# An attention layer with its heads padded on the key side: GpSimd pads K, Q is one dense add, the causal mask joins the maximum on VectorE

## The chip, the cores and the metric

The kernel runs on one core of one Trainium2 chip. The metric is the time of one execution on the device, in microseconds (us); lower is better. Five engines run their own queues of instructions in order: TensorE (PE, with its weight loads shown as PEld), VectorE (DVE), ScalarE (ACT), GpSimd (POOL) and SyncE (SP), which issues most DMAs. They meet at semaphores.

## What is computed

A residual stream `x` of 4 batches of 1024 tokens of 128 features goes through six layers: mixture of experts, a two-way state-space layer, mixture of experts, a ternary gated network, causal attention, the ternary network again. The change is inside the attention layer alone. Cut to what matters, that layer is

```python
# x: 4 batches, 1024 tokens, 128 features; 16 heads of 8 features
q, k, v = split(layernorm(x) @ w_in.T + b_in)      # each to heads: (batch, 16, 1024, 8)
scores = einsum('bhqd,bhkd->bhqk', q / sqrt(8), k) + causal_bias   # 0 or -inf
out = einsum('bhqk,bhkd->bhqd', softmax(scores), v)
x = x + out.reshape(batch, 1024, 128) @ w_out.T + b_out
```

All of it is in float32; the projections are taken in three matmul passes with the operands split into a rounded high part and a low rest.

## The kernel before, in words

The attention layer is the function `attention` (L1781). It handles the 16 heads in 4 groups of 4 heads, batch after batch: 16 group turns in all, and a turn is called a slot here. A head has 8 features, and its row block on the 128 partitions is 32 rows: 8 rows of the rounded part, 8 twice for the rest, and rows that carry the row maximum. Four heads together fill 128 rows, so a matmul over 128 rows would mix the four heads. To keep them apart one of the two operands holds zeros in the rows of the other three heads. In the kernel before that operand is Q: `Q` has one 1024-column block per head (16 of them), `K` has one dense block per group.

A slot is 12 steps (`STEPS`), v = 0 to 11. Each step has four units, one a head:

- PE's `exp_unit` (L2008, matmul L2018) makes the transposed scores of group g into one of three PSUM buffers, ACT's `exp_unit` (L2109, L2116) takes the exponential, POOL's `mask_step` (L2354, L2357 and L2360) zeroes the triangle in the eight steps on the diagonal (v = 0 to 3 and 8 to 11), and PE's `value_step` (L2022, L2034) of the step before multiplies by V, between the second and third unit.
- The pass for the row maximum of the next group runs beside it: PE's `max_unit` (L1994, matmul L2002) makes scores into one of three other buffers, DVE's `max_unit` (L2207, L2216) reduces them. On the diagonal chunks, 32 of the 48 units of a slot, a second matmul (L2005) adds -1e30 above the diagonal: identity times mask, 128 columns. A PE unit waits until the third unit before it has been read by ACT or DVE.
- After its four units a step may have one further use of the single PSUM bank `M` (`slot_uses` L1812, `m_use` L2037): at v = 0 and 2 the projection of Q of the group after next, at 4 and 5 that of K, at 6 that of V, at 1 and 7 the transposed row maxima ("max"), at 3 and 9 the normalisation of the output. A use waits until the one before has been read out of `M`.

Q and K come out of `M` as two ACT instructions (`qf` L2135, `qh` L2138) and one on DVE (`stack`, L2283). K lands dense in `K`. Q lands in the scratch `stk`, and ACT's `queries` (L2147, L2155) copies it to the padded `Q`: four instructions of 32 partitions for each half of 512 columns, placed in the steps v = 9 and 10, one after each exponential. The zeros of `Q` are written once ahead of the layer: by one POOL memset (L2332) and three DMAs (L2330). "max" adds the row maxima to `Q`, in the DVE function `m_read` (L2225): four instructions of 32 partitions x 512 (L2238), two between each pair of units of steps 2 and 8.

The order on each engine is written out by `all_slots` (L1897): a stage "pre" that has the maximum pass of group 0 only, a stage "first" for batch 0, a loop `Fori` for batches 1 and 2, "last" for batch 3, and "tail". Before the slots POOL fills constants and computes two reciprocal roots (`rstd_of`, L2322).

## Time and profile before

| | us |
|---|---|
| time, median of 3 runs | 2952.7 (2952.65 to 2961.28) |
| span of the profiled execution | 3037.0 |
| attention layer in it, without its tail | 1973.0 to 2757.5 |
| of that, the pass for the first maximum | 2002.4 to 2034.0 |
| the 16 slots | 2034.0 to 2757.5 |
| PE, DVE, ACT, POOL busy over the whole span | 2549.4, 2285.1, 1790.3, 1373.7 |

The profile gives no time of that execution beyond its span, so what lies around the span is in no row; the comparison goes span against span and median against median. Times in the trace are counted from the start of the span. A duration that a row shows is that of an instruction from its start to its end; instructions of one engine overlap a little, so that the distance from start to start is shorter. A busy PE is a modelled time. "Idle before, releaser" tells how long an engine stood still before an instruction and what it was that ended the wait.

### The profile page before, as it was taken

To read this page: it belongs to the slowest core of one execution; us is meant where nothing else is said; L and a number is where in the kernel's file an instruction comes from. 1 tells how busy PE (TensorE), PEld (TensorE's weight loads), DVE (VectorE), ACT (ScalarE), POOL (GpSimd) and SP (SyncE) were. 2 spreads that over 40 slices of the span, in tenths; PEclk is the share of its full clock that TensorE was granted. 3 is DMA by queue.
4 is the path that set the end of the run, shared out by engine and by line. 5 is a ranking of instruction groups with operands and counts; after the bars stand their busy time and mean duration, and the time that the engine had idled before them with its cause. 6 is when DMAs were issued, how large, how long until landed. Compare 5 with 4: busy or idle time off the path is not lost. (4 is left out here: it accounts for less than half of the span.)

```text
span 3037.0 us, 38397 instructions
## 1 busy us (share of the span) xinstructions
PE 2549.4 (84%) x11128; PEld 1669.2 (55%) x11128; DVE 2285.1 (75%) x3877; ACT 1790.3 (59%) x3099; POOL 1373.7 (45%) x1486
## 2 busy tenths in 40 slices
PE   6888477888888888868887689969988889887999
PEld 5766233343344344227676568746555556554887
DVE  6887478989999999998786544478777777774444
ACT  3566465657556656524666445547777667665555
POOL 2365488888988988961563630021121121111000
PEclk9999688999999999998998789979999999998999
DMA  2246222222222222221345200020000000001000
GB/s 69 55 130 123 79 68 67 75 69 72 70 74 74 77 73 74 77 71 39 75 130 96 73 21 1 0 95 1 1 1 1 2 1 1 1 1 39 7 8 14
DMA packets 99804, 152.38 MB, mean 50 GB/s; under 512 B 12940, under 2 KB 50572, under 8 KB 99028
## 3 DMA queue, kind: packets, MB, share of 16 engines
q1 hardware_dynamic: 82052, 98.41, 10.6%
q0 software_dynamic: 17040, 51.07, 6.8%
q8 instruction: 91, 1.49, 0.2%
q14 instruction: 109, 0.89, 0.1%
q10 hardware_dynamic: 512, 0.53, 0.1%
HBM read 131.08 MB, written 18.87 MB: 49 GB/s over the span
## 5 line engine op out<-in xcount | busy, mean ns | idle before, releaser
L1750 POOL TENSOR_TENSOR a_hc<-a_H,a_cb 128x512 f32<-128x512 f32 x512 | 620.0, 1233 | 134.3 <-DVE a_H L1614 127.3
L1406 PE MATMUL a_Y<-a_hc,ident 128*128 128x512 f32 x1024 | 535.3, 633 | 57.0 <-POOL a_hc L1750 48.6
L2216 DVE TENSOR_REDUCE a_mx<-a_W 128x1 f32<-128x512 f32 (+3 forms) x768 | 397.2, 550 | 153.3 <-PE a_W L2005 99.6
L2116 ACT ACTIVATE a_pt<-a_W 128x512 f32<-128x512 f32 (+3 forms) x768 | 353.5, 493 | 224.1 <-PE a_W L2018 220.7
L1532 ACT ACTIVATE a_dA<-a_dt,a_aneg 128x512 f32<-128x512 f32 x512 | 342.6, 714 | 193.8 <-POOL a_dt L1769 103.2
L1406 PEld LDWEIGHTS a_Y<-a_hc,ident 128*128 128x128 f32 x1024 | 183.0, 196 | 307.6 <-POOL a_hc L1750 212.7
L1638 DVE TENSOR_TENSOR a_BX<-a_u,a_BX 128x1024 f32<-128x1024 f32 x256 | 308.6, 1211 | 44.0 <-PE a_BX L1340 22.3
L1614 DVE TENSOR_TENSOR_SCAN a_H<-a_dA,a_H,a_BX 128x512 f32<-128x512 f32 x256 | 312.5, 1264 | 2.5 <-ACT a_dA L1532 2.5
L2018 PE MATMUL a_W<-a_Q,a_K 128*128 128x512 f32 (+3 forms) x768 | 302.3, 399 | 4.1 <-ACT a_pt L2116 2.0
L1614 DVE TENSOR_TENSOR_SCAN a_H<-a_dA,a_BX 128x512 f32<-128x512 f32 x256 | 296.7, 1202 | 1.1 <-POOL a_hc L1750 1.0
L2002 PE MATMUL a_W<-a_K,a_Q 128*128 128x512 f32 (+3 forms) x768 | 273.9, 363 | 20.4 <-DVE a_K L2283 9.9
L2357 POOL TENSOR_TENSOR a_spare<-a_zero 128x1 f32<-128x1 f32 x128 | 27.8, 217 | 578.9 <-ACT a_pt L2116 578.9
L1340 PE MATMUL a_BX<-a_bcs,a_sel 128*128 128x512 f32 x256 | 173.9, 680 | 96.4 <-DVE a_H L1614 82.6
L715 POOL DMA_INDIRECT m_xg<-m_xrows,m_gidx x184 | 190.1, 1033 | 120.9 <-DVE m_didx L599 65.4
L1046 DVE TENSOR_TENSOR t_hl<-t_raw,t_hh 128x512 fp32r<-128x512 f32 x128 | 87.5, 691 | 203.1 <-ACT t_hh L947 184.2
L2018 PEld LDWEIGHTS a_W<-a_Q,a_K 128*128 128x128 f32 x768 | 145.8, 192 | 142.0 <-issue 68.8
L441 ACT ACTIVATE m_raw<-m_U,m_wg 128x512 f32<-128x512 f32 x248 | 172.6, 697 | 82.6 <-PE m_U L335 48.0
L609 DVE TENSOR_TENSOR m_hl<-m_raw,m_hh 128x512 fp32r<-128x512 f32 x248 | 171.1, 692 | 56.4 <-ACT m_hh L445 30.7
L2034 PE MATMUL a_PV<-a_pt,a_V 128*32 128x512 f32 (+3 forms) x1536 | 167.0, 507 | 42.4 <-POOL a_pt L2360 41.3
L842 PE MATMUL t_U<-t_hh,t_wh 128*128 128x512 f32 x512 | 201.4, 393 | 0.0
L844 PE MATMUL t_U<-t_hl,t_wh 128*128 128x512 f32 x512 | 199.5, 390 | 0.0
L843 PE MATMUL t_U<-t_hh,t_wl 128*128 128x512 f32 x512 | 199.3, 389 | 0.0
(327 smaller groups left out, 5628.4 us busy)
## 6 DMA issues: line engine op xcount, KB each, us to landing
a_cb<-a_crow SPq DMA_DIRECT2D x256, 256.0 KB, 3.1
m_orows<-m_yt SPq DMA_DIRECT2D x46, 256.0 KB
a_Q<-attention_zeros POOLq DMA_DIRECT2D x3, 2048.0 KB, 13.3
t_wst<-ternary_w SPq DMA_DIRECT2D x22, 256.0 KB, 2.7
m_xrows<-m_pool SPq DMA_DIRECT2D x16, 256.0 KB, 2.3
m_xg<-m_xrows,m_gidx POOLq DMA_INDIRECT x184
out<-x SPq DMA_DIRECT2D x8, 256.0 KB, 2.3
m_wg<-moe_ws SPq DMA_DIRECT2D x2, 516.0 KB, 4.5
```

The source lines that it names most:

```text
L842: pe.matmul(out, wh[:, piece, c], rhs_h, start=start, stop=False)
L843: pe.matmul(out, wl[:, piece, c], rhs_h, start=False, stop=False)
L844: return pe.matmul(out, wh[:, piece, c], rhs_l, start=False, stop=stop)
L1406: pe.matmul(Y[:, h, :], ident[:], hc[:, g % HCRING, :], start=False, stop=v == NS - 1).then_inc(s_y, 1)
L1532: act.activation(dA[:, G % ARING, :], dt[:, b % 2, h, :], ACT.Exp, scale=aneg[:, d, h, v:v + 1]).then_inc(s_dA, 1)
L1614: dve.tensor_tensor_scan(out, a, bb, init, ALU.mult, ALU.add).then_inc(s_scan, 1)
L1638: dve.tensor_tensor(both_banks(Q), u[:, b % 2, :, :], BX[:, row_bank(Q), :].unsqueeze(1).broadcast_to([P, HALF, BLK]), ALU.mult).then_inc( ...
L1750: pool.tensor_tensor(hc[:, G % HCRING, :], H[:, s, span], cb[:, v % RING, :], ALU.mult).then_inc(s_hc, 1)
L2002: mm = pe.matmul(out, Q[:, g * GH + j, tile(t)], K[:, g, c * BLK:c * BLK + cols], start=True, stop=not diag)
L2018: pe.matmul(W[:, 3 + u % 3, 0:BLK - r * P], K[:, g, tile(kt)], Q[:, g * GH + j, c * BLK + r * P:(c + 1) * BLK], start=True, stop=True).the ...
L2116: act.activation(pt[:, u % PR, 0:BLK - r * P], W[:, 3 + u % 3, 0:BLK - r * P], ACT.Exp).then_inc(s_exp, 1)
L2216: dve.tensor_reduce(dst, W[:, s % 3, 0:min(BLK, (t + 1) * P - c * BLK)], AX, ALU.max)\
```

## The change

The two operands swap roles. `K` becomes the padded one (16 blocks) and `Q` the dense one (4 blocks).

- The projection order swaps: K at v = 0 and 2, Q at v = 4 and 5. K now goes through `stk`, Q lands in `Q`.
- POOL pads K: for each half of 512 columns four `tensor_scalar` of 128 x 512, each multiplying `stk` by a column that is 1 in the rows of one head and 0 elsewhere, and by 1.0. They stand after the masks of steps 2 and 3 (two each, the first half) and after the split of the next group's maxima (four, the second half). Eight of them stand in POOL's queue before it splits the first maxima, and eight more for group 1.
- ACT's copies L2155 go. The memset L2332 and the DMAs L2330 go.
- "max" is one DVE add of 128 x 512 to `Q` instead of four of 32 x 512.
- On the diagonal the second matmul L2005 goes. DVE adds the mask and takes the maximum in one `tensor_tensor_reduce`, which also writes the masked scores to a scratch `masked`. The mask is loaded 512 columns wide (384 of zeros before the triangle) instead of 128. Off the diagonal DVE's `tensor_reduce` stays.
- The `Fori` loop becomes a Python loop: batches 1 and 2 are written out.

The diff, cut to its core:

```diff
-            uses.update({-7: ("xT", 0, 0, 0), -6: ("xT", 0, 0, 1), -5: ("Q", 0, 0, 0), -4: ("Q", 0, 0, 1),
-                         -3: ("K", 0, 0, 0), -2: ("K", 0, 0, 1), -1: ("V", 0, 0, 0)})
+            uses.update({-7: ("xT", 0, 0, 0), -6: ("xT", 0, 0, 1), -5: ("K", 0, 0, 0), -4: ("K", 0, 0, 1),
+                         -3: ("Q", 0, 0, 0), -2: ("Q", 0, 0, 1), -1: ("V", 0, 0, 0)})
...
-            uses.update({0: ("Q", rel, n, 0), 2: ("Q", rel, n, 1), 4: ("K", rel, n, 0), 5: ("K", rel, n, 1),
+            uses.update({0: ("K", rel, n, 0), 2: ("K", rel, n, 1), 4: ("Q", rel, n, 0), 5: ("Q", rel, n, 1),
...
-        with eng.Fori(1, NBATCH - 1) as i:
+        for i in range(1, NBATCH - 1):
...
-                    out = W[:, s % 3, 0:cols]
-                    mm = pe.matmul(out, Q[:, g * GH + j, tile(t)], K[:, g, c * BLK:c * BLK + cols],
-                                   start=True, stop=not diag)
-                    if diag:
-                        mm = pe.matmul(W[:, s % 3, cols - P:cols], idr[:], mneg[:], start=False, stop=True)
-                    mm.then_inc(s_S, 1)
+                    pe.matmul(W[:, s % 3, 0:cols], Q[:, g, tile(t)], K[:, g * GH + j, c * BLK:c * BLK + cols],
+                              start=True, stop=True).then_inc(s_S, 1)
...
-                    pe.matmul(W[:, 3 + u % 3, 0:BLK - r * P], K[:, g, tile(kt)],
-                              Q[:, g * GH + j, c * BLK + r * P:(c + 1) * BLK],
+                    pe.matmul(W[:, 3 + u % 3, 0:BLK - r * P], K[:, g * GH + j, tile(kt)],
+                              Q[:, g, c * BLK + r * P:(c + 1) * BLK],
...
-                                    pe.wait_ge(s_q, 2 * G + 4)
+                                    pe.wait_ge(s_k, 2 * G + 4)
...
-                            copied = copies(stage, g, v)
-                            if copied:
-                                queries(i, copied, j)
...
+                    if last:
+                        dve.tensor_tensor_reduce(masked[:, s % 3, 0:cols], W[:, s % 3, 0:cols], mask[:, BLK - cols:],
+                                                 1.0, LEAST, ALU.add, ALU.max, dst).then_inc(s_max, 1)
+                    else:
+                        dve.tensor_reduce(dst, W[:, s % 3, 0:cols], AX, ALU.max).then_inc(s_max, 1)
...
-                    if kind == "max" and j < 2:
-                        for jj in (2 * j, 2 * j + 1):
-                            q = Q[head(jj), n * GH + jj, chunk(c)]
-                            ins = dve.tensor_tensor(q, q.bitcast(F32), M[head(jj), :], ALU.add)
-                        if j == 1:
-                            last = ins
+                    if kind == "max" and j == 0:
+                        q = Q[:, n, chunk(c)]
+                        last = dve.tensor_tensor(q, q.bitcast(F32), M[:], ALU.add)
...
-                for dst, src in ZEROS:
-                    pool.dma_start(dst, src).then_inc(s_zero, 16)
                 pool.wait_ge(s_xn, 1)
-                pool.memset(Q[:, 0:GH, :].bitcast(F32), 0.0).then_inc(s_cst, 1)
...
+                def keys(G, n, c, js):
+
+                    if js[0] == 0:
+                        pool.wait_ge(s_ld, 16 * len(LOADS))
+                        pool.wait_ge(s_st, 4 * G + c + 1)
+                    for j in js:
+                        last = pool.tensor_scalar(K[:, n * GH + j, chunk(c)], stk[:, c, :].bitcast(F32),
+                                                  heads[:, j:j + 1], 1.0, ALU.mult, ALU.mult)
+                    if js[-1] == GH - 1:
+                        last.then_inc(s_k, 1)
+
                 def slot(stage, i, g):
                     G = i * GROUPS + g
+                    n = (g + 2) % GROUPS
+                    ahead = stage not in ("last", "tail") or (stage == "last" and g + 2 < GROUPS)
+                    if stage == "pre":
+                        keys(0, 0, 0, range(GH))
+                        keys(0, 0, 1, range(GH))
+                        keys(1, 1, 0, range(GH))
+                        keys(1, 1, 1, range(GH))
                     if has_exp(stage):
                         split_max(stage, i, g, G, g, 1)
                         for v in DIAG[:TPB]:
                             mask_step(i, g, v)
+                            if ahead and v >= 2:
+                                keys(G + 2, n, 0, range(2 * (v - 2), 2 * (v - 1)))
                     if has_max(stage, g):
                         split_max(stage, i, g, G + 1, (g + 1) % GROUPS, 0)
                     if has_exp(stage):
+                        if ahead:
+                            keys(G + 2, n, 1, range(GH))
                         for v in DIAG[TPB:]:
                             mask_step(i, g, v)
```

## Rows read from the trace of the kernel before

**Rows 1.** First maximum pass: stretch, us, busy PE, PEld, DVE, ACT, POOL, clock, DMA.
```profile
2002.40:2034.00 31.60, 27.58 (x109) 20.68 (x109) 28.38 (x59) 11.98 (x17) 0.99 (x3) 0.75 0.00 1
```

**Rows 2.** The same view of two single slots, the seventh and the eighth.
```profile
2306.20:2350.30 44.10, 39.69 (x267) 26.30 (x265) 34.89 (x71) 32.66 (x67) 8.28 (x22) 1.00 0.01 2
2350.30:2397.00 46.70, 40.39 (x266) 26.60 (x264) 35.52 (x72) 32.45 (x67) 9.85 (x27) 0.96 0.01 2
```

**Rows 3.** Waits in the 16 slots: waiter, releaser: us in total, times, longest.
```profile
PEld a_W L2018 <- ACT a_pt L2116: 62.8, 92, 1.2
PEld a_PV L2034 <- POOL a_pt L2360: 58.6, 70, 1.5
PEld a_M L1990 <- DVE a_Q L2238: 17.1, 14, 2.2
```

**Rows 4.** Groups of DVE by shape: busy us, mean ns, idle before.
```profile
L2216 DVE TENSOR_REDUCE a_mx<-a_W 128x1 f32<-128x512 f32 x384 | 247.4, 680 | 74.6 <-PE a_W L2002 50.5 <-PE a_W L2005 23.6
L2238 DVE TENSOR_TENSOR a_Q<-a_Q,a_M 32x512 fp32r<-32x512 f32 x128 | 87.2, 681 | 8.2 <-PE a_M L2063 6.3
L1614 DVE TENSOR_TENSOR_SCAN a_H<-a_dA,a_BX 128x512 f32<-128x512 f32 x256 | 296.7, 1202 | 1.1 <-POOL a_hc L1750 1.0
L2283 DVE SCALAR_TENSOR_TENSOR a_stk<-a_qh,a_low,a_qf 128x512 f32<-128x512 f32 x32 | 28.4, 887 | 1.8 <-ACT a_qh L2138 1.4
L2222 DVE TENSOR_TENSOR a_mx<-a_mx 128x4 f32<-128x4 f32 x64 | 12.0, 187 | 1.0
```

**Rows 5.** Groups by shape on ACT, PE and POOL.
```profile
L2155 ACT ACTIVATE a_Q<-a_stk 32x512 fp32r<-32x512 f32 x128 | 80.1, 626 | 5.7 <-DVE a_stk L2283 3.1
L2005 PE MATMUL a_W<-a_mneg,a_idr 128*128 128x128 f32 x512 | 123.3, 241 | 0.0
L2360 POOL TENSOR_SCALAR_AFFINE_SELECT a_pt<-a_pt 128x512 f32<-128x512 f32 x128 | 87.2, 681 | 0.0
L1750 POOL TENSOR_TENSOR a_hc<-a_H,a_cb 128x512 f32<-128x512 f32 x512 | 620.0, 1233 | 134.3 <-DVE a_H L1614 127.3 <-PE a_Y L1406 6.0
```

**Rows 6.** Timeline of DVE: start, us (all of the row's instructions), what.
```profile
2314.22 1.36 DVE L2238 TENSOR_TENSOR a_Q<-a_Q,a_M 32x512 fp32r<-32x512 f32 x2
2315.91 1.39 DVE L2238 TENSOR_TENSOR a_Q<-a_Q,a_M 32x512 fp32r<-32x512 f32 x2
...
2390.14 2.48 DVE L2216 TENSOR_REDUCE a_mx<-a_W 128x1 f32<-128x512 f32 x4 [0.57 <-PE a_W L2002]
```

**Rows 7.** Timeline of PE, pieces of the seventh slot; the last row opens the ninth.
```profile
2316.14 0.22 PE L2002 MATMUL a_W<-a_K,a_Q 128*128 128x128 f32 x1
2316.20 0.27 PE L2005 MATMUL a_W<-a_mneg,a_idr 128*128 128x128 f32 x1
2317.36 0.50 PE L1990 MATMUL a_M<-a_xh,a_wh 128*128 128x512 f32 x1 [0.89 <-DVE a_Q L2238]
...
2340.62 1.06 PE L2034 MATMUL a_PV<-a_pt,a_V 128*32 128x512 f32 x8
...
2344.65 0.85 PE L2034 MATMUL a_PV<-a_pt,a_V 128*32 128x384 f32 x8 [0.76 <-POOL a_pt L2360]
...
2345.89 0.28 PE L2018 MATMUL a_W<-a_Q,a_K 128*128 128x256 f32 x1
...
2348.73 0.64 PE L2034 MATMUL a_PV<-a_pt,a_V 128*32 128x256 f32 x8 [1.24 <-POOL a_pt L2360]
...
2397.04 0.79 PE L2018 MATMUL a_W<-a_Q,a_K 128*128 128x512 f32 x1 [1.94 <-issue]
```

**Rows 8.** Timeline of ACT in steps 9 and 10 of the seventh slot.
```profile
2342.09 0.49 ACT L2116 ACTIVATE a_pt<-a_W 128x384 f32<-128x384 f32 x1 [0.73 <-PE a_W L2018]
...
2343.25 0.49 ACT L2116 ACTIVATE a_pt<-a_W 128x384 f32<-128x384 f32 x1
...
2347.43 0.39 ACT L2116 ACTIVATE a_pt<-a_W 128x256 f32<-128x256 f32 x1
```

**Rows 9.** Timeline of POOL ahead of the slots.
```profile
1992.98 4.20 POOL L2326 TENSOR_TENSOR a_rstd<-a_veps,a_mhalf 128x24 f32<-128x24 f32 x1
```

More of the change, by code:

```diff
@@ L1795, in attention @@
     ROWS = P // GH
+    LEAST = -3.0e38
     NCH, TPS = SEQ // BLK, SEQ // P
@@ L1846, in attention @@
             for st, gs in SLOTS.items()}
-    def copies(stage, g, v):
-        uses = slot_uses(stage, g)
-        use = uses.get(v - 2) if v < 0 else uses.get({9: 0, 10: 2}.get(v))
-        return use if use and use[0] == "Q" else None
     WEIGHT = {"M": lambda k: 1, "D": lambda k: k not in ("Q", "K", "oT"), "A": lambda k: k in ("Q", "K", "oT"),
@@ L1920, in attention @@
         wo, bo = sb("wo", [P, P]), sb("bo", [P, P])
-        mask = sb("mask", [P, P])
-        idr, mneg = sb("idr", [P, P], F32R), sb("mneg", [P, P], F32R)
-        stk = sb("stk", [P, 2, BLK])
+        mask, heads = sb("mask", [P, BLK]), sb("heads", [P, GH])
+        masked = sb("masked", [P, 3, BLK])
+        stk = sb("stk", [P, 2, BLK], F32R)
         mhalf, zero = sb("mhalf", [P, TILES]), sb("zero", [P, TPB, GH])
@@ L1961, in attention @@
                  (scale[:], w["scale"]), (low[:], w["low"]), (wo[:], w["w_out"]), (bo[:], w["b_out"]),
-                 (mask[:], w["mask"]))
-        ZEROS = tuple((Q[:, n:n + GH, :].rearrange("p h c -> p (h c)"), w["zeros"].bitcast(F32R))
-                      for n in range(GH, GROUPS * GH, GH))
+                 (mask[:], w["mask"]), (heads[:], w["heads"]))
         def early(v):
@@ L2097, in slot @@
                             m_use(stage, i, g, v, uses[v])
-                all_slots(slot, pe)
+                all_slots(slot)
             @block.scalar
@@ L2105, in _ @@
                 act.activation(wvh[:], wvs[:], ACT.Copy).then_inc(s_wh, 1)
-                act.activation(idr[:], ident[:], ACT.Copy)
-                act.activation(mneg[:], mask[:], ACT.Copy).then_inc(s_pre, 1)
                 def exp_unit(i, g, v, j):
@@ L2145, in m_read @@
                             act.activation(oT[:, c, :], M[:], ACT.Copy).then_inc(s_Ma, 1)
-                def queries(i, use, j):
-                    if isinstance(i, int) and i == 0 and use[2] == 1 and j == 0:
-                        act.wait_ge(s_zero, 16 * len(ZEROS))
-                    kind, rel, n, c = use
-                    G = (i + rel) * GROUPS + n
-                    if j == 0:
-                        act.wait_ge(s_st, 4 * G + c + 1)
-                    last = act.activation(Q[head(j), n * GH + j, chunk(c)], stk[head(j), c, :], ACT.Copy)
-                    if j == GH - 1:
-                        last.then_inc(s_q, 1)
                 def slot(stage, i, g):
@@ L2275, in stack @@
                     G = (i + rel) * GROUPS + n
-                    m, k = (c, n) if kind == "Q" else (2 + c, GROUPS + n)
+                    m, k = (c, GROUPS + n) if kind == "K" else (2 + c, n)
                     dve.wait_ge(s_Ma, through("A", stage, i, g, v))
-                    if kind == "Q":
-                        wait(dve, s_q, 2 * (G - 1) + c + 1)
+                    if kind == "K":
+                        wait(dve, s_k, 2 * (G - 1) + c + 1)
                         out = stk[:, c, :]
                     else:
-                        out = K[:, n, chunk(c)]
+                        out = Q[:, n, chunk(c)]
                     dve.scalar_tensor_tensor(out, qh[:, m % 2, :].bitcast(F32), low[:, k:k + 1],
@@ L2313, in _ @@
                 chain = [None]
-                all_slots(slot, dve)
+                all_slots(slot)
             @block.gpsimd
@@ L2525, in attention_layout @@
         "w_out": g("w_out").T, "b_out": np.broadcast_to(g("b_out"), (P, P)),
-        "mask": np.triu(np.full((P, P), -1e30, np.float32), 1), "zeros": np.zeros((P, 4096), np.float32),
+        "mask": np.pad(np.triu(np.full((P, P), -1e30, np.float32), 1), ((0, 0), (3 * P, 0))), "heads": np.repeat(np.eye(GH, dtype=np.float32), ROWS, 0),
     }
```

27 lines of the change are left out of this document (12 added, 15 removed).

## The prediction

> **What bounds the kernel now.** Nothing outside the attention layer changes, so only its 784 us count, and of these the 16 slots are 723.5 us. I read busy time by stretch first. In a slot of 44.1 us PE is busy 39.7, DVE 34.9, ACT 32.7 and POOL 8.3 [rows 2]. No engine is full, PE is nearest, and its clock is at the upper of its levels, 2.4 GHz, for the whole slot. So the slot is a chain that runs through the engines in turn, and the waits tell where PE stands still. Over the 16 slots it waits 62.8 us for ACT's exponentials, 58.6 for POOL's triangle mask, which follows them, and 17.1 for DVE's adds to Q, in 14 places [rows 3]. The timeline shows the two places:
>
> - In step 2 the last mask matmul starts at 2316.20 and the next projection at 2317.36, because DVE needs until 2317.3 for four adds with reductions between them [rows 6, 7].
> - In steps 9 and 10 the value matmuls wait for POOL's mask; POOL waits for the step's fourth exponential, and that one stands on ACT behind copies of Q, one after each exponential [rows 5, 7, 8].
>
> **The change part by part.** All prices are per slot and from start to start where the rows allow it.
>
> *Mask matmuls.* 32 go. The next matmul starts 0.06 us after a 128-column one [rows 7], so they cost PE 32 x 0.057 = 1.8 us; the 0.241 us of the group is length, not cost [rows 5]. Half of them (steps 0, 1, 3, 6) stand where PE never waits: 0.9 us kept. The others lie in the waits counted next.
>
> *The adds to Q.* Four instructions of 0.68 us become one of 128 x 512; its DVE time goes by the columns, not by the partitions, so it is priced like one of the four [rows 4, 6]. DVE gets back 2 x 3 x 0.69 = 4.1 us. On the path: bank M is read at 2314.22 + 0.68 = 2314.90 instead of 2317.30. The projection of step 2 then follows its last score matmul at about 2316.26: 1.1 us kept. In step 8 the same adds hold a score matmul, but the value matmul behind it waits for POOL's mask anyway, which comes from exponentials that are not touched: 0.3 us kept.
>
> *ACT's copies.* Eight of 0.626 us go [rows 5], 5.0 us of ACT. On the path: in step 9 the fourth exponential starts 2343.25 and the third 2342.09. Without the copy between them it starts 0.5 later than the third, at 2342.6: 0.65 us earlier, and with it mask and value matmul (2344.65). In step 10 the fourth exponential starts at 2347.43, though its scores were started at 2345.89. The lag from score matmul to exponential without a queue is about 0.47 (2341.62 is the score matmul's start after the value matmul of 2340.62 and its 1.0 us; the exponential follows at 2342.09 [rows 7, 8]), so it could start at 2346.36. That is 1.07 earlier, and the value matmul of 2348.73 moves with it. What comes late next there is DVE: four reductions take 2.48 us [rows 6], and between two value matmuls there are four of them and the small operations of the normalisation, 2.9 us, against the 3.0 that the chain then takes. So these are kept, but no more. Sum 1.7 us.
>
> *The fused instruction.* 32 reductions become `tensor_tensor_reduce`, and the trace has no such instruction. From below: nothing extra, since a two-operand DVE instruction of 512 columns takes 681 ns and a reduction 680 [rows 4]. From above: the scan, also a two-operand instruction with a running result, takes 1202 ns at the same width. I take 0.10 us extra for each, near the lower end, because a running maximum is what the reduction does already, four of 512 columns in 2.48 us [rows 6]. That is 3.2 us of DVE, less than the 4.1 that the adds give back. It hides in DVE's idle time (9 us a slot), except in steps 9 to 11 and at chain ends: 0.5 us lost.
>
> *POOL's padding.* Eight instructions of 128 x 512 with one tensor input. Bounds: the triangle mask, one input, 0.68 us, and a product of two tensors, 1.23 us [rows 5]. I take 0.75, near the one-input row: 6 us, on an engine busy 8.3 of 44.1 us. Queued behind the first two, and behind their wait for `stk`, is the mask of step 3, on which PE's value matmul waits. `stk` is written by the end of step 1 and padded after the mask of step 2, so that wait is over before it starts. The masks of steps 2 and 3 are ready some 3.5 us apart; two paddings take 1.5, so nothing. The other six fall between steps 3 and 8, when POOL has nothing else but the split of the maxima, used at step 7 at the earliest: nothing. If a padding took 1.23, the mask of step 3 would be up to 0.7 us late.
>
> Sum for a slot: 0.9 + 1.1 + 0.3 + 1.7 - 0.5 = 3.5 us. It holds for the 14 slots that have projections and copies: 49.0 us. The fifteenth has neither and keeps 1.0, the last has no maximum pass and keeps about 1.1 through the adds.
>
> *The loop.* The eighth slot ends with the loop's back edge. It takes 46.7 us instead of 44.1, and PE stands 1.94 us at the start of the ninth for nothing that the profile shows [rows 2, 7]. The clock is 0.96 there, so part is the clock's. Bounds 1.9 and 4.2 (the slow first step after it included); I take 3.0. Entering the loop costs nothing visible, and batches 0 and 3 are straight code already with slots of the same length, so fetching more code is put at nothing.
>
> *Ahead of the slots.* The memset, the zero DMAs and ACT's eight copies go, but POOL's queue now holds the first keys: its reciprocal roots end at 1997.2 [rows 9], and eight paddings of 0.75 put the first score matmul at 2003.2, against 2002.4 now: 1.0 lost (range 0 to 4.7). The first maximum pass is DVE's own, 28.4 of 31.6 us [rows 1]: 32 x 0.10 added, three adds of 0.69 and the lag of the mask matmuls taken away, 0.5 lost. The larger mask to load may delay the first projections by under 1 us; they wait later for the statistics anyway.
>
> Total: 49.0 + 1.0 + 1.1 + 3.0 - 1.0 - 0.5 = 52.6 us. Against the profiled execution that is 3037.0 - 52.6 = 2984 us of span. That execution is 2.8% longer than the median; the difference is taken over unscaled, as scaling it would change it by 1.5 us: 2952.7 - 52.6 = 2900 us.
>
> **Rivals.**
>
> *The fused instruction costs like two.* The nearest row for a second small instruction is the 4-column maximum, 187 ns [rows 4]. Then DVE gets 6.0 us more in a slot against 4.1 less, and 1.5 instead of 0.5 us come to lie on the path; the first pass loses 2.9 more. 2900 + 14 + 3 = 2917. For it: the instruction has two results. The Trainium skill says just this, in "VectorE: DVE Perf Modes", section "Two Vector instructions with no wait between them": an operation that also writes out its accumulator is two instructions, the main one and the read of the accumulator. No row here shows such a pair.
>
> *GpSimd is slow.* 1.23 us a padding: 14 x 0.7 + 8 x 0.48 = 14 us, 2914. Against it: the mask, also one input, takes 0.68.
>
> *The fused instruction runs at half rate (slower than before).* Priced like the scan it costs 0.58 us more at 512 columns, and by the 10240 diagonal columns of a slot 11.6 us: DVE has 34.9 - 4.1 + 11.6 = 42.4 us of work, bunched where the diagonal units are wide. Steps 11, 0 and 1 have 4 x 1.2 + 4 x 1.2 + 4 x 0.9 = 13.2 us of it against 10.9 that these steps last, and what the other steps gain is eaten by DVE's starts behind the value matmuls. I put the slot at 45.6, 1.5 more than now, which is 22 us; the first pass 6.5 more; the loop 3.0 less: 2978. It decides from about 1.1 us for 512 columns. For it: the scan's row [rows 4]. Against it: the reduction runs at full rate. The Trainium skill stands against it too, in "DVE: opcode table, instruction layouts, handler registers and perf-mode slots", section 6: a stage that reads its own last result has no bubble, and only a result carried back to an earlier stage, as in the scan, halves the rate; the 1202 and 680 ns of the two rows agree.
>
> *The freed time is idle time.* PE is 90% busy, and what DVE and ACT no longer do may only lengthen their waits; then the kernel keeps the loop and some mask matmuls, 8 us in all: 2945. Against it: the two chains above are seen, wait by wait.
>
> **How the numbers follow.** Forecast 0.58; a gain beyond it (nothing for the fused instruction, all mask matmuls kept, the loop at 4.2: 4.9 us a slot, 2870) 0.04; two instructions 0.13; GpSimd slow 0.12; half rate 0.08, of which 0.01 ends near no change; idle time 0.05. A measurement of this kernel tells 0.3%, 8.9 us, from no change. Faster 0.87, same 0.06, slower 0.07. Range: low 2868, the case beyond; high 2930, two instructions and slow padding together. Outside it are the half rate and the idle case.
>
> **What would show it.** In the profile after: the step-2 projection directly behind the last score matmul; `exp` back to back in steps 9 and 10 and PE's waits for POOL down from 58.6 to some 30 us; the fused instruction within 0.7 to 0.8 us at 512 columns; a padding at 0.65 to 0.85; first score matmul near 2003; slots of 40 to 41 us. Wrong if the fused instruction takes over 0.9 us, if PE's waits for POOL grow, or if slots stay at 44.

## The result and the profile after

The changed kernel takes 2872.9 us (median of 4 runs, 2870.1 to 2875.5), the kernel before 2955.3 beside it: ratio 0.972, 95% interval 0.971 to 0.974. That is 82.4 us less, where 52.6 were forecast. The time lies inside the range (2868 to 2930), at its low end.

The profiled execution of before was longer than its median, and the excess lies in the stages ahead of attention, which take about 84 us more in it and in every run of two of the three sets of experiments below, whatever the kernel; so only stretches within attention are compared here, and experiments are set against a kernel that ran beside them.

Within attention the stages read as follows. The start, from GpSimd's first memset to the first score matmul, went from 28.7 to 30.3 us (1.7 lost, 1.0 forecast). The first maximum pass went from 31.6 to 29.5 (2.1 gained, 0.5 lost was forecast). The 16 slots went from 723.5 to 641.3: 82.2 gained. In this view the rows are the first maximum pass, the seventh slot, the eighth, and all sixteen; the first three answer to [rows 1, 2].

```profile
1916.06:1945.60 29.54, 25.75 (x77) 16.48 (x77) 26.40 (x87) 7.07 (x9) 5.98 (x11) 0.73 0.00 0
2191.30:2230.90 39.60, 36.87 (x235) 22.21 (x234) 30.26 (x97) 27.30 (x59) 13.61 (x30) 1.00 0.01 1
2230.90:2270.20 39.30, 36.55 (x234) 22.14 (x233) 29.57 (x96) 26.96 (x59) 13.83 (x30) 1.00 0.00 1
1945.60:2586.90 641.30, 583.86 (x3697) 352.22 (x3695) 466.31 (x1476) 426.43 (x923) 206.88 (x460) 0.99 0.00 1
```

The seventh slot lost 4.5 us of its 44.1. PE is now busy 36.9 of 39.6, DVE 30.3 (34.9 before), ACT 27.3 (32.7), and POOL 13.6 (8.3), which has taken the padding. The eighth is shorter by 7.4, since the loop's back edge has gone with it.

The groups of DVE and POOL that answer to [rows 4, 5]:

```profile
L2186 DVE CUSTOM_DVE_ANT_0 a_masked<-a_W,a_mask 128x512 f32<-128x512 f32 x128 | 82.8, 686 | 9.5 <-PE a_W L1991 8.0
L2186 DVE DVE_READ_ACCUMULATOR2_ANT a_mx<- 128x1 f32 x512 | 42.2, 82 | 0.0
L2189 DVE TENSOR_REDUCE a_mx<-a_W 128x1 f32<-128x512 f32 x256 | 166.7, 680 | 50.4 <-PE a_W L1991 48.0
...
L2335 POOL TENSOR_SCALAR a_K<-a_stk,a_heads 128x512 fp32r<-128x512 f32 x128 | 86.5, 691 | 7.9 <-DVE a_stk L2252 7.8
L2326 POOL TENSOR_SCALAR_AFFINE_SELECT a_pt<-a_pt 128x512 f32<-128x512 f32 x128 | 95.3, 744 | 0.0
```

The fused instruction has a second record, the read of its accumulator. Whether that costs anything is read from starts, not from durations. DVE's timeline, around the seam of the seventh and the eighth slot (start, us):

```profile
2229.22 0.68 DVE L2186 CUSTOM_DVE_ANT_0 a_masked<-a_W,a_mask 128x512 f32<-128x512 f32 x1
2229.83 0.08 DVE L2186 DVE_READ_ACCUMULATOR2_ANT a_mx<- 128x1 f32 x1
2229.83 0.69 DVE L2186 CUSTOM_DVE_ANT_0 a_masked<-a_W,a_mask 128x512 f32<-128x512 f32 x1
2230.44 0.08 DVE L2186 DVE_READ_ACCUMULATOR2_ANT a_mx<- 128x1 f32 x1
```

The next fused instruction starts in the same hundredth as the read, 0.61 us after the one before it. Plain reductions of this width follow each other at 0.60 to 0.62 (four in 2.48 in [rows 6]). So the mask is free on DVE, to 0.01 us. The same holds at 128, 256 and 384 columns, where the shortest distances from start to start are 0.21, 0.34 and 0.47 us here and 0.20, 0.33 and 0.46 for the reduction before.

PE's and ACT's timelines in the seventh slot, and POOL's ahead of the slots, which answer to [rows 7 to 9]:

```profile
2200.70 0.22 PE L1991 MATMUL a_W<-a_K,a_Q 128*128 128x128 f32 x1
2200.75 0.45 PE L1981 MATMUL a_M<-a_xh,a_wh 128*128 128x512 f32 x1
...
2223.32 1.06 PE L2020 MATMUL a_PV<-a_pt,a_V 128*32 128x512 f32 x8 [0.74 <-POOL a_pt L2326]
...
2229.43 0.64 PE L2020 MATMUL a_PV<-a_pt,a_V 128*32 128x256 f32 x8 [0.17 <-POOL a_pt L2326]
```

ACT:

```profile
2221.32 1.85 ACT L2100 ACTIVATE a_pt<-a_W 128x512 f32<-128x512 f32 x4 [0.75 <-PE a_W L2004]
...
2227.78 1.27 ACT L2100 ACTIVATE a_pt<-a_W 128x256 f32<-128x256 f32 x4 [1.16 <-PE a_W L2004]
```

POOL:

```profile
1906.05 4.48 POOL L2295 TENSOR_TENSOR a_rstd<-a_veps,a_mhalf 128x24 f32<-128x24 f32 x1
1910.63 5.37 POOL L2335 TENSOR_SCALAR a_K<-a_stk,a_heads 128x512 fp32r<-128x512 f32 x8
```

The projection of step 2 stands 0.05 us behind the last score matmul (1.16 before). The value matmul that waited 1.24 us before waits 0.17. The last row of ACT holds the third and fourth exponential of step 10 and the first two of step 11, back to back: the fourth of step 10 starts 0.35 us after the third, 1.05 before. In step 9 the distance is 0.38 (1.16 before). One line goes against the forecast, PE's waits in the 16 slots:

```profile
PEld a_PV L2020 <- POOL a_pt L2326: 64.1, 103, 1.3
PEld a_W L2004 <- ACT a_pt L2100: 62.2, 98, 0.8
```

By its weight loads, which is what [rows 3] count, PE waits for POOL's triangle mask no less than before (58.6 us in 70 places) but more, in more places. A weight load can wait while PE is still busy with the matmuls in front of it, so this is not all lost time: a load that waited 0.31 us at 2231.89 has no wait before its matmul. By the matmuls themselves the wait fell, first before, then after:

```profile
PE a_PV L2034 <- POOL a_pt L2360: 41.3, 47, 1.3
PE a_PV L2020 <- POOL a_pt L2326: 31.6, 48, 1.1
```

### The profile page after: what moved, and what is told of

It reads as the page before. It is cut to its first block and busy times, and to the rows that moved or that the text cites. A ratio compares the mean times of both kernels' runs of the same rounds, so it can differ in the third digit from the quotient of the medians.

```text
span 2868.1 us, 35851 instructions
## 1 busy us (share of the span) xinstructions
PE 2465.1 (86%) x10616; PEld 1578.1 (55%) x10616; DVE 2215.6 (77%) x4293; ACT 1698.2 (59%) x2969; POOL 1453.1 (51%) x1610
## 5 line engine op out<-in xcount | busy, mean ns | idle before, releaser
L2100 ACT ACTIVATE a_pt<-a_W 128x512 f32<-128x512 f32 (+3 forms) x768 | 345.6, 494 | 225.9 <-PE a_W L2004 221.9
L2186 DVE CUSTOM_DVE_ANT_0 a_masked<-a_W,a_mask 128x384 f32<-128x384 f32 (+3 forms) x512 | 233.8, 487 | 101.6 <-PE a_W L1991 98.5
L2004 PE MATMUL a_W<-a_Q,a_K 128*128 128x512 f32 (+3 forms) x768 | 282.3, 384 | 2.0 <-ACT a_pt L2100 2.0
L1991 PE MATMUL a_W<-a_K,a_Q 128*128 128x512 f32 (+3 forms) x768 | 264.8, 360 | 14.3 <-POOL a_K L2335 10.6
L2189 DVE TENSOR_REDUCE a_mx<-a_W 128x1 f32<-128x512 f32 x256 | 166.7, 680 | 50.4 <-PE a_W L1991 48.0
```

Source lines behind the costliest of these rows:

```text
L1991: pe.matmul(W[:, s % 3, 0:cols], Q[:, g, tile(t)], K[:, g * GH + j, c * BLK:c * BLK + cols], start=True, stop=True).then_inc(s_S, 1)
L2004: pe.matmul(W[:, 3 + u % 3, 0:BLK - r * P], K[:, g * GH + j, tile(kt)], Q[:, g, c * BLK + r * P:(c + 1) * BLK], start=True, stop=True).the ...
L2100: act.activation(pt[:, u % PR, 0:BLK - r * P], W[:, 3 + u % 3, 0:BLK - r * P], ACT.Exp).then_inc(s_exp, 1)
L2186: dve.tensor_tensor_reduce(masked[:, s % 3, 0:cols], W[:, s % 3, 0:cols], mask[:, BLK - cols:], 1.0, LEAST, ALU.add, ALU.max, dst).then_in ...
```

## The experiments

The yardstick in what follows is a slot in which nothing but the slot's own work happens: no loop edge, no output projection, the upper clock throughout. I call it a quiet slot and read it from the starts of the exponentials' score matmuls: the fourth, the eighth and the twelfth, where they are undisturbed. It is 44.15 us before and 39.34 after, 4.8 less, and those of one kernel agree within 0.07 us. (The third and the seventh of the changed kernel are 0.2 longer. The second, third, fourth and seventh, which nothing disturbed in either kernel, gained 4.7 on average.) Each run is judged by it and by its time.

**One part undone: the mask back on TensorE.** `u2_pemask`

```
-                    pe.matmul(W[:, s % 3, 0:cols], ..., start=True, stop=True).then_inc(s_S, 1)
+                    mm = pe.matmul(W[:, s % 3, 0:cols], ..., start=True, stop=not diag)
+                    if diag:
+                        mm = pe.matmul(W[:, s % 3, cols - P:cols], idr[:], mneg[:], start=False, stop=True)
...
-                    if last:
-                        dve.tensor_tensor_reduce(masked[...], W[...], mask[...], 1.0, LEAST, ALU.add, ALU.max, dst)
+                    dve.tensor_reduce(dst, W[:, s % 3, 0:cols], AX, ALU.max).then_inc(s_max, 1)
```

> The changed kernel (2872.9 us) with the mask back on TensorE: the second matmul of 128 columns on the diagonal, and tensor_reduce on VectorE everywhere. Theory A (the slot is a chain PE, ACT, POOL's triangle mask, PE; a matmul costs only in steps where PE never waits): steps 0 and 1 lose 0.3 us each, others little, 0.6 to 0.9 us a slot, about +12 us: 2885. Rival B (PE is the bound at 90% busy, each matmul costs its 0.057 us): 32 x 0.057 x 15 = 27 us: 2900. Rival C (the fused instruction is dearer than a reduction, so undoing it gains): under 2873.

Measured: 2883.3 us (2882.4 to 2884.0), 10.4 above the changed kernel, as A has it; B and C fall. Its seventh slot by the view of stretches, then PE's wait over its 16 slots by weight loads and by matmuls, then its reductions:

```profile
2195.80:2236.00 40.20, 39.25 (x268) 26.31 (x266) 31.00 (x65) 27.77 (x59) 13.04 (x30) 1.00 0.01 1
```

```profile
PEld a_PV L2024 <- POOL a_pt L2328: 36.2, 86, 1.4
PE a_PV L2024 <- POOL a_pt L2328: 12.7, 20, 1.2
```

```profile
L2191 DVE TENSOR_REDUCE a_mx<-a_W 128x1 f32<-128x512 f32 x384 | 247.3, 680 | 53.5 <-PE a_W L1992 41.3 <-PE a_W L1995 11.6
```

A quiet slot is 40.12: the mask on DVE is worth 0.78. The wait for POOL is 36.2 us here and 64.1 in the changed kernel by weight loads, 12.7 and 31.6 by matmuls, and in the seventh slot PE stands still 1.0 us here and 2.7 there. So the matmuls removed, 1.8 us of PE in a slot, leave PE early at POOL's mask, and most of what they free turns into this wait. Steps 0, 1, 4, 8 and 11 are shorter in the changed kernel by 0.33, 0.23, 0.23, 0.43 and 0.18, while step 2 is 0.47 longer (3.74 against 3.27).

Step 2 has a second reason. The value matmul in it reads the triangle mask of step 1, and in the changed kernel that mask takes 1.16 us instead of 0.63. It starts while DVE's instruction that writes `stk`, which reads two full tensors from SBUF, is running. In `u2_pemask` the two start together and it is DVE's that takes longer. In the kernel before the same mask starts only as `stk` ends, 0.6 us late. The eighth slot of the changed kernel (DVE, POOL, and PE's wait behind it), then that of `u2_pemask` (DVE, POOL):

```profile
2237.48 0.75 DVE L2252 SCALAR_TENSOR_TENSOR a_stk<-a_qh,a_low,a_qf 128x512 fp32r<-128x512 f32 x1
2237.57 1.16 POOL L2326 TENSOR_SCALAR_AFFINE_SELECT a_pt<-a_pt 128x512 f32<-128x512 f32 x1
2238.78 0.85 PE L2020 MATMUL a_PV<-a_pt,a_V 128*32 128x384 f32 x8 [1.05 <-POOL a_pt L2326]
```

```profile
2243.10 1.17 DVE L2254 SCALAR_TENSOR_TENSOR a_stk<-a_qh,a_low,a_qf 128x512 fp32r<-128x512 f32 x1
2243.10 0.63 POOL L2328 TENSOR_SCALAR_AFFINE_SELECT a_pt<-a_pt 128x512 f32<-128x512 f32 x1
```

The 0.52 us that this mask loses are as large as the 0.47 of step 2. That is read from rows and not isolated: `d10_extra` below has no long mask, and its step 2 takes 3.68 us, but its DVE does more work in that step.

**One part undone: four adds to Q.** `u3_adds`

```
-                    if kind == "max" and j == 0:
-                        q = Q[:, n, chunk(c)]
-                        last = dve.tensor_tensor(q, q.bitcast(F32), M[:], ALU.add)
+                    if kind == "max" and j < 2:
+                        for jj in (2 * j, 2 * j + 1):
+                            q = Q[head(jj), n, chunk(c)]
+                            ins = dve.tensor_tensor(q, q.bitcast(F32), M[head(jj), :], ALU.add)
```

> The changed kernel with the row maxima added to Q by four VectorE instructions of 32 partitions instead of one of 128. Theory A: the projection of step 2 waits again for the bank, 1.3 us a slot, and step 8 or 9 loses 0.3: 1.6 x 14 + 2 = +24 us: 2897. Rival D (VectorE has idle time enough, 29% of a slot, and the gain came from the copies and the mask): within 5 us of 2873.

Measured: 2916.0 us (2914.2 to 2918.9), 43 above the changed kernel: more than A, and D falls. Its eighth slot by the view of stretches, then in the timelines of DVE and of PE's weight loads:

```profile
2253.20:2294.30 41.10, 36.91 (x234) 22.30 (x233) 33.70 (x102) 26.99 (x59) 13.82 (x30) 1.00 0.00 1
```

```profile
2260.69 1.36 DVE L2210 TENSOR_TENSOR a_Q<-a_Q,a_M 32x512 fp32r<-32x512 f32 x2
2262.40 1.39 DVE L2210 TENSOR_TENSOR a_Q<-a_Q,a_M 32x512 fp32r<-32x512 f32 x2
```

```profile
2263.84 0.19 PEld L1981 LDWEIGHTS a_M<-a_xh,a_wh 128*128 128x128 f32 x1 [1.42 <-DVE a_Q L2210]
```

The wait of step 2 is back. A quiet slot is 41.09, 1.75 longer: 1.5 in step 2, 0.3 in step 9. Fourteen of these are 24.5 us; the first maximum pass gives 3.9 more (33.3 against 29.5). Of the remaining 15, 8 lie in the seventh, tenth and eleventh slot, where the clock fell to 0.50 in this profile and not in that of the changed kernel (27.7 us of the first 15 slots against 9.5). About 2 lie in the fifth, ninth and thirteenth, at the full clock. More on both below.

**One part undone: K padded by ACT.** `u4_actcopy`

```
-                            if ahead and v >= 2:
-                                keys(G + 2, n, 0, range(2 * (v - 2), 2 * (v - 1)))
...
+                    last = act.activation(K[head(j), n * GH + j, chunk(c)], stk[head(j), c, :].bitcast(F32), ACT.Copy)
...
+                            if copied:
+                                queries(i, copied, j)
```

> The changed kernel with K padded by ScalarE: four copies of 32 partitions for each half, in steps 9 and 10, into zeros that a memset and three DMAs write once; GpSimd pads nothing. Theory A: the fourth exponentials of steps 9 and 10 come late again, steps 8 to 11 lose 1.7 to 2.2 us a slot in 14 slots, +24 to +31 us, less 1 to 2 us at the start: about 2899. Rival E (each copy costs what ScalarE spends on it, 5.0 us a slot): +70 us: 2943. Rival F (GpSimd's padding costs as much as it saves, through the triangle mask behind it): within 5 us of 2873.

Measured: 2903.0 us (2897.7 to 2905.3), 30 above the changed kernel, A's number; E and F fall. ACT's timeline in step 10 shows the queue in which the exponentials stood:

```profile
2284.52 0.62 ACT L2147 ACTIVATE a_K<-a_stk 32x512 fp32r<-32x512 f32 x1
2285.17 0.38 ACT L2108 ACTIVATE a_pt<-a_W 128x256 f32<-128x256 f32 x1
2285.58 0.63 ACT L2147 ACTIVATE a_K<-a_stk 32x512 fp32r<-32x512 f32 x1
2286.12 0.36 ACT L2108 ACTIVATE a_pt<-a_W 128x256 f32<-128x256 f32 x1
```

A quiet slot is 41.48, 2.14 longer: 0.76 in step 10 and 1.24 in step 11, where the value matmuls of steps 9 and 10 stand, and 0.14 elsewhere. The three parts sum to 0.78 + 1.75 + 2.14 = 4.67 of the 4.8: they are additive, and nothing else of size is in the slot. POOL's paddings cost a slot nothing that shows: steps 2 to 9 last the same to 0.04 us with them and without.

**One part alone: the loop written out.** `b9_unrolled`

```
-        with eng.Fori(1, NBATCH - 1) as i:
+        for i in range(1, NBATCH - 1):
```

> The kernel before with nothing changed but the batch loop written out. Theory A: only the one back edge goes, 3 to 4.3 us: 2951 against 2955. Rival G (waits against a register's value and the address arithmetic of the loop body cost time all along the two middle batches, so that the loop is worth a tenth of the 82 us or more): 2945 or less. Rival H (more code to fetch): slower than 2955.

Measured: 2953.1 us against 2953.8 beside it, ratio 0.999 (0.997 to 1.001). At its place the back edge is seen to go: the last step of the eighth slot takes 4.01 in place of 6.76 us, 2.75 less. In the total it is not seen, and the interval is too wide to show it: 34.1 us of the first 15 slots run at the lower clock in this profile, 27.3 before. G and H fall.

**Two parts alone.** `b5_unrolled_fused` is the kernel before with the loop written out and the fused instruction.

```
-                        with eng.Fori(1, NBATCH - 1) as i:
+        for i in range(1, NBATCH - 1):
...
+                        dve.tensor_tensor_reduce(masked[...], W[...], mask[:, BLK - cols:], 1.0, -3.0e38, ALU.add, ALU.max, dst)
```

> The kernel before with the batch loop written out and the mask added by VectorE in the maximum instruction; Q is still padded by four adds, and ACT still copies K. Theory A (the parts add up: an undisturbed slot of the changed kernel with the mask on TensorE is 0.78 us longer): 16 x 0.78 = 12 us for the mask and its share in the first maximum pass, and what writing out the loop gave, 0 to 4 us: 12 to 16 us, 2937 to 2942 us. Rival S (the mask's gain needs the VectorE time that the single add frees): no more than 5 us, 2948 us or above.

Measured: 3027.4 us against 3035.5 beside it, ratio 0.997 (0.996 to 0.999): 8 us less, between A's 12 to 16 and S's 5. Its best slot, the one quiet slot in which the clock stayed up, is 43.1 us, 1.0 under before, which agrees with 39.34 + 1.75 + 2.14 = 43.2. So the mask's gain per quiet slot doesn't need the DVE time that the adds free, and S falls as a mechanism. In the total most of it is not seen: 54.7 us of the first 15 slots run at the lower clock in this profile, 27.3 before. (ACT copies Q in this kernel, not K.)

**What the fused instruction would have cost.** `d10_extra`

```
+        extra = sb("extra", [P, 4, 64])
...
+                        dve.tensor_tensor(extra[:, s % 4, :], mask[:, 0:64], mask[:, 0:64], ALU.add)
```

> The changed kernel with one more small VectorE instruction (two inputs, 64 columns, about 0.13 us) behind each of the 32 fused maximum instructions of a slot: 4.2 us of VectorE a slot, as the rival 'costs like two instructions' had priced them. It tells whether the price of the fused instruction lay on the path. The prediction's own working (1.5 of 6.0 us on the path of a slot): 1.0 us a slot and 4.2 us in the first maximum pass, 15 + 4 = 19 us, 2892 us. Rival N (VectorE's idle time hides it in the slots): 4 us, 2877 us. Rival X (VectorE is the bound now): all of it, 67 us, 2940 us.

Measured: 2976.3 us, with before at 3035.5 beside it. The changed kernel, run again in the next set with before at 3033.7 beside it, took 2954.0 (`a0_changed`, below): 22 us more. DVE's timeline:

```profile
2332.14 0.28 DVE L2187 CUSTOM_DVE_ANT_0 a_masked<-a_W,a_mask 128x128 f32<-128x128 f32 x1
2332.34 0.08 DVE L2187 DVE_READ_ACCUMULATOR2_ANT a_mx<- 128x1 f32 x1
2332.34 0.21 DVE L2189 TENSOR_TENSOR a_extra<-a_mask 128x64 f32<-128x64 f32 x1
2332.48 0.28 DVE L2187 CUSTOM_DVE_ANT_0 a_masked<-a_W,a_mask 128x128 f32<-128x128 f32 x1
```

Where the next instruction can follow, the extra one costs 0.14 us from start to start, 4.5 us of DVE in a slot; by busy time DVE has 6.1 more (35.7 against 29.6 in the eighth slot). A quiet slot grows by 0.88 to 40.22, the first pass by 2.9. N and X fall. Between a fifth (of 4.5) and a seventh (of 6.1) of what DVE gets in addition lies on the path. Fourteen slots and the first pass make 15 of the 22 us; of the rest most lies in the sixth, tenth and fourteenth slot, in which the clock fell further or more often than in `a0_changed`. The prediction had put it at a sixth (0.5 of 3.2) and for the dear case at a quarter (1.5 of 6.0). Its share was sound; its price of 0.10 us was not.

**What PE's wait for POOL is worth.** Four kernels, run beside `a0_changed` or one set earlier. `m7_thinmask` leaves 120 of 128 columns of each diagonal tile unmasked; `v8_value_j2` and `v9_value_j3` compute all and move PE's value matmuls behind the third or the fourth unit; `m8_both` is the thin mask with the third unit.

```
-                    d = pt[:, (v % 2) * GH:(v % 2 + 1) * GH, 0:P]
+                    d = pt[:, (v % 2) * GH:(v % 2 + 1) * GH, 0:8]
```

> The changed kernel, but GpSimd's triangle mask of the exponentials covers 8 of the 128 columns of each tile (so 120 columns of the diagonal tiles stay unmasked and the output is another); everything else is as in the changed kernel. It tells what the chain exponential, mask, value matmul is still worth. In the changed kernel TensorE waits 31.6 us in the 16 slots for this mask by its matmul records, and the mask takes 0.74 us. Theory P (these waits are TensorE's own idle time, and the four exponentials end early enough that the mask alone is late): nearly all of it goes, 25 to 32 us, 2841 to 2848 us. Theory R (behind the mask stands ACT's exponential and the three banks of scores, which hold TensorE a moment later): 8 to 15 us go, 2858 to 2865 us.

```
-                            if j == 1 and v > 0 and has_exp(stage):
+                            if j == 2 and v > 0 and has_exp(stage):
...
-                            if j == 1 and v == 0 and stage != "pre" and (stage, g) != ("first", 0):
+                            if j == 2 and v == 0 and stage != "pre" and (stage, g) != ("first", 0):
```

> The changed kernel, but the value matmuls of the step before are issued behind the third unit of a step and not behind the second, so that two more score matmuls (0.3 to 0.5 us) lie between the mask and its first reader. Theory P (TensorE stands only because it comes too early to the mask): its waits for the mask, 31.6 us in 48 places, shrink by 0.3 to 0.5 us each, 14 to 24 us, 2849 to 2859 us. Theory R (the score matmuls that would fill the wait need a bank that an exponential or a maximum has not read yet, so the wait moves in front of them): within 5 us of the changed kernel, 2868 to 2878 us; if the value matmuls are then late for the normalisation, slower.

> The changed kernel itself, beside the other three, so that their times can be set against it on one chip. Every theory expects an undisturbed slot of 39.35 us and a first padding group of 5.4 us, and 82 us (75 to 90) less than the kernel before.

> The changed kernel with the value matmuls of the step before behind the fourth unit of a step (behind the second in the changed kernel; behind the third an undisturbed slot took 37.94 us in place of 39.35). Theory P (TensorE merely comes too early): no wait for the mask is left, the slot ends at TensorE's own work, 37.1 to 37.6 us, 25 to 32 us under the changed kernel. Theory R (what the value matmuls give free, the banks and VectorE's normalisation, now comes late): 37.9 us or longer, no better than 20 us under the changed kernel.

> The changed kernel with the value matmuls behind the third unit and with the triangle mask over 8 of 128 columns (120 columns of the diagonal tiles stay unmasked, another output). Each alone brought an undisturbed slot from 39.35 to 37.94 and 37.77 us. Theory P (both remove the same wait, TensorE's for the mask): together hardly more than one, 37.4 to 37.8 us a slot, 20 to 27 us under the changed kernel. Theory T (two separate waits): the gains add up, 36.4 us, 40 us or more under it.

Measured, in us; the last column is against `a0_changed`, and for `m7` and `v8` across two sets whose kernel before agrees within 1.8:

```
              time     quiet slot   against the changed kernel
a0_changed   2954.0     39.32
m7_thinmask  2930.2     37.77        -24
v8_value_j2  2939.3     37.94        -15
v9_value_j3  2918.2     37.25        -36
m8_both      2921.2     37.27        -33
```

`a0_changed` gives 79.7 us under before and the quiet slot of the first set. In `m7` the mask takes 0.28 us in place of 0.74. It comes near P, `v8` is P's number, and both fall outside R. `m8` lies between P and T: the two remove the same wait, and each a little that the other leaves. `v9` exceeds its P. In it no wait for the mask is left among the large ones. Its eighth slot by the view of stretches, PE's timeline in it, and the largest of PE's waits for another engine in the 16 slots:

```profile
2296.80:2334.00 37.20, 36.51 (x233) 22.37 (x233) 29.19 (x98) 26.75 (x58) 12.96 (x30) 1.00 0.00 1
```

```profile
2330.14 0.50 PE L1991 MATMUL a_W<-a_K,a_Q 128*128 128x512 f32 x1
2330.57 0.85 PE L2020 MATMUL a_PV<-a_pt,a_V 128*32 128x384 f32 x8
```

```profile
PEld a_W L2004 <- ACT a_pt L2100: 28.0, 63, 0.8
```

The value matmul follows the score matmul with nothing between, and PE is busy 36.5 of 37.2. POOL's mask and DVE's `stk` hardly meet any more either: one of its 128 masks lasts over 0.8 us, against 27 in the changed kernel. This version beats both kernels: ratio to before 0.961 (0.958 to 0.965), where the changed kernel beside it has 0.973 (0.969 to 0.977).

**A dearer padding.** `p7_padprod`

```
-                        last = pool.tensor_scalar(K[...], stk[...], heads[:, j:j + 1], 1.0, ALU.mult, ALU.mult)
+                        last = pool.tensor_tensor(K[...], stk[...], heads[:, j:j + 1].to_broadcast([P, BLK]), ALU.mult)
```

> The changed kernel, but each padding of K on GpSimd is a product of two tensors (the column of zeros and ones broadcast), the instruction whose 1.23 us stood as the upper bound. It is the rival 'GpSimd is slow' made true. By the prediction's working: 8 x 0.5 = 4 us ahead of the first score matmul, and up to 0.7 us a slot in step 3, where the mask stands behind two paddings: 14 us together over the changed kernel. Theory C (VectorE, ACT and TensorE never feel it in the slots, GpSimd is busy 13.8 of 39.4 us): 4 us, all of it ahead of the slots, and an undisturbed slot of 39.35 us. Theory L (the mask stands late in more steps than one, since TensorE waits for it already in four places of a slot): 20 us or more, and step 3 longer by over 0.7 us.

```profile
L2335 POOL TENSOR_TENSOR a_K<-a_stk,a_heads 128x512 fp32r<-128x512 f32 x128 | 130.2, 1044 | 6.9 <-DVE a_stk L2252 6.9
```

Measured: 2961.7 us, 7.7 above `a0_changed`, where the runs of each spread over 11 to 12 us. The product took 1.04 us, not 1.23, so the rival's own price was not reached. Ahead of the slots the start is about 2.7 us longer (eight paddings in 8.03 in place of 5.37), and a quiet slot is 39.54, 0.2 longer, 0.16 of it in step 4 (3.54 against 3.38). There the value matmul that reads step 3's mask stands, so the prediction's place was right (the expectation's "in step 3" was a slip), and its 0.7 us, worked out for 1.23, was about four times too much for 1.04. The whole is between C and the prediction's 14; L falls.

The loop put back into the changed kernel was not tried; its worth there stays what `b9_unrolled` says of the kernel before.

## Why the prediction was right, and where it was small

The sign, the place and most of the mechanisms held; the size did not, and that the time still fell into the range was luck in part, as the end of this section says. In order of its sum:

- *Mask matmuls and fused instruction*: 0.9 - 0.5 = 0.4 us a slot forecast, 0.78 measured. The 0.9 was nearly right in size and not in place. Steps 3 and 6, two of the four in which the matmuls were to be kept whole, gain nothing; step 4, which has none of them, gains 0.23; and of the 1.4 that steps 0, 1, 4, 8 and 11 gain, step 2 takes back 0.47. The 0.5 was wrong, from a price of 0.10 us that is 0.01. The term "a running maximum is what the reduction does already" should have been taken to its end. The Trainium skill, "VectorE: DVE Perf Modes", section "Two Vector instructions with no wait between them", says that an operation that writes out its accumulator is two instructions. The trace agrees, with 82 ns for the second, but the pair costs no more than one, since the next main instruction starts with the read.
- *Adds to Q*: 1.1 + 0.3 forecast, 1.75 measured, 1.5 of it in step 2. The 0.3 shows in step 9, not 8. The term was priced with the mask matmuls in place; without them PE comes earlier to the same four adds, and they cost it more: it waits 21.0 us for them in `u3_adds`, 17.1 before [rows 3].
- *ACT's copies*: 0.65 + 1.07 forecast, 0.76 + 1.24 and 0.14 elsewhere measured. The claim that no more than these are kept, because DVE comes late next, was close.
- *Padding*: 0.75 forecast, 0.69 long and 0.67 from start to start. Nothing in the slots, as forecast.
- *Start and first pass*: -1.0 and -0.5 forecast, -1.7 and +2.1 measured. Of the 1.7 only 0.3 lie behind the reciprocal roots, where the paddings stand; 1.4 came ahead of them, and why is open. The second is the price of the fused instruction again: 32 x 0.10 had been charged and 2.0 us of DVE went [rows 1].
- *Fifteenth slot*: 1.0 forecast, 4.0 measured. `u2_pemask` shows 1.3 of it for the masks alone (36.5 against 35.1) and `u3_adds` 0.9 for the adds (36.0); of the other 1.8 the most is a fall of the clock in before.
- *Loop*: 3.0 forecast, 2.75 at its place.

The 4.7 of an undisturbed slot instead of 3.5 makes 17 us of the missing 30; the fifteenth slot 3, the first pass 2.6, the start -0.7. Of the remaining 8 or so the record shows two parts that the sum did not have.

The first, about 3.4 us, is at the full clock. The fifth and the thirteenth slot gained 5.8 and 6.0 us (46.00 and 46.17 before, 40.17 and 40.13 after), 1.1 more than a quiet slot, and the ninth is of the same kind. In these three bank `M` is also used at step 8, for the output, so that before the four adds held PE there as they do at step 2: step 8 took 4.46 us and takes 2.91, and with the four adds back it is 4.36 (`u3_adds`). The sixth, tenth and fourteenth slot use it there too, but the clock or more work for the output disturbs them; together they gained 15.7 us, 1.3 more than three quiet slots. The sum priced all fourteen like the seventh.

The second is the clock. In the 15 slots up to the last, 27.3 us of before ran at 0.50 and 9.5 us of the changed kernel, 2.7 of these as the end of a stretch that began in the first pass. Four stretches of before, about the start of the twelfth slot; the figure behind POOL's is the clock:

```profile
2533.60:2537.00 3.40, 2.15 (x17) 1.22 (x16) 2.31 (x4) 2.58 (x8) 0.78 (x2) 0.99 0.01 2
2537.00:2540.40 3.40, 3.40 (x13) 2.58 (x12) 2.24 (x4) 1.51 (x4) 1.41 (x5) 0.50 0.00 0
...
2547.20:2550.60 3.40, 1.92 (x15) 1.16 (x16) 3.30 (x8) 0.72 (x2) 1.17 (x3) 1.00 0.00 0
2550.60:2554.00 3.40, 3.40 (x18) 2.17 (x17) 1.07 (x4) 1.79 (x4) 0.00 (x0) 0.50 0.00 0
```

Ahead of each fall to 1.2 GHz PE had stood still for a good part of the stretch, busy 2.15 and 1.92 us of 3.40. The first is the wait of 1.2 us behind ACT's copies; in the second stand the two waits of step 2, 0.7 us for POOL and 1.0 for DVE. The changed kernel has neither the first nor the wait for DVE, and no fall in these slots. But the waits alone do not bring a fall: the seventh slot has them all, and its clock is 1.00 [rows 2]. The eleventh and twelfth slot took 44.7 and 46.5 us with these two stretches, undisturbed ones 44.1 each: 1.5 us for each stretch. The second slot of `b9_unrolled` lost 2.4 us with two, 1.2 for each. In all there are eight such stretches before and two after. One of the eight lies at the loop's edge and one in the fifteenth slot, which are counted above; by that price the other four fewer give 5 to 6 us, less 1 for the 2.7 us in the first slot of the changed kernel. That is worked out, not isolated: no run changes the clock alone, and kernels with nearly the same waits (before and `b9_unrolled`) differ by 7 us at the lower clock in one profile each.

One forecast of the profile was wrong outright: PE's waits for POOL, counted by weight loads as in [rows 3], were to fall from 58.6 to some 30 us, and they are 64.1; by matmuls they fell from 41.3 to 31.6. The fall did come, to 36.2 (12.7 by matmuls), in the kernel that has the other two parts alone (`u2_pemask`). The mask matmuls were taken for lost time or nothing, and what they are is a filler: PE comes 1.8 us earlier to the same POOL mask, and waits. The prediction had seen this for the steps with known waits, not for step 2, where a wait for POOL of 0.8 before is 1.05 in the eighth slot after. Half of that one is the mask itself, which DVE's `stk` holds up by 0.52 us. The prediction read the mask's 681 ns as the length of each; it is a mean of most at 637 and 12 of 128 at 1.1 us and more. "Wrong if PE's waits for POOL grow" was a bad sign to set: by weight loads they grew while the time fell.

Of the rivals, "two instructions" was true in the records and not in the time; "half rate" fell with the 0.61 us; "GpSimd slow" and "idle time" with the slots. The case "beyond the forecast" (2870) has come true in its number, 4.8 us a quiet slot for its 4.9, and in nothing for the fused instruction; its other two conditions have not: the mask matmuls give 0.78 of their 1.8, and the loop 2.75, not 4.2. The adds, the copies, the slots that use bank `M` at step 8 and the clock made up for them. Its chance of 0.04 was small for the fused instruction alone being free. Its sum is off as well: taken over fourteen slots, as the forecast is, the case gives about 2875, and 2870 is what 4.9 over sixteen slots and the loop's 4.2 give. The measured 2872.9 lies below that, so the lower end of the range, drawn at this case, held it by luck.

## What to carry to other kernels

Cost the parts of a change in a slot free of disturbances, then look which slots are of another kind before multiplying. A stall can cost twice, once itself and once in the clock behind it. Take a wait for lost time only where the matmul waits, not its weight load, and look behind a mean: two instructions that hold each other up show as a few long ones. When work is taken off the busiest engine, ask at which wait it will now arrive early. The answer names the next edit, here the value matmuls moved behind two more units, worth 36 us beside the change's 80.

## What of the hardware was not expected

- `tensor_tensor_reduce` with a mask takes 686 ns at 128 x 512 and 0.61 us from start to start, within 0.01 of the plain reduction; its accumulator read of 82 ns is hidden. The scan, also with a running result, takes 1202.
- GpSimd pads 128 x 512 with a column as scalar in 0.67 us, eight in 5.37. As a product with a broadcast column it takes 1.00 (eight in 8.03), where a product of two full tensors takes 1.23 [rows 5].
- GpSimd's triangle mask and DVE's instruction that writes `stk` hold each other up. The mask's mean went from 681 to 744 ns and that of `stk` from 887 to about 760, but the mask's median stayed at 635 to 637. In the changed kernel 27 of 128 masks last 1.09 to 1.18 us; all 27 start while a `stk` instruction is running, and each ends 0.49 us behind it. In `u2_pemask` no mask is long, and 28 of the 32 `stk` instructions last 1.17 to 1.21 us, each ending 0.54 us behind a mask. Before, 12 masks and 13 `stk` instructions are long. DVE's reductions from PSUM run beside a mask without such a loss.
- Code written out in place of a loop cost nothing in the slots that can be seen, and gave 2.75 us at the edge.
